# A graph transformer layer on one core: Gram product of the upper block triangle with transposed copies below, and a tail with its work spread anew over four engines

## What is computed

```python
xn = layernorm(x)
x = x + gnn(xn, edges) + mix(xn)
x = x + ffn(layernorm(x))

def mix(x):                     # no softmax: linear attention over all nodes
    q, k, v = x @ Wq.T + bq, x @ Wk.T + bk, x @ Wv.T + bv
    return (q @ k.T * scale) @ v @ Wo.T + bo

def ffn(x):                     # each operand rounded to fp4 in blocks of 16
    gate, up = lin4(x, gate_w), lin4(x, up_w)
    return lin4(silu(gate) * up, down_w)
```

## Time and profile before

| | us |
|---|---|
| median of 3 runs | 1122.34 (1117.62 to 1124.64) |
| the profiled execution | 1125.02 |
| its span, first to last instruction | 1123.0 |
| PE busy | 970.6 (86%) |
| DVE busy | 869.0 (77%) |
| POOL busy | 593.5 (53%) |
| ACT busy | 532.4 (47%) |

### The profile page before, as it was taken

One profiled execution on the slowest core, in us unless ns is written; L12 is line 12 of the kernel. 1 busy time (PEld: TensorE's weight loads), 2 busy tenths in 40 slices (PEclk: granted clock), 3 DMA queues, 4 the chain that ended last, 5 costly groups with the idle time before them and its releaser, 6 DMA issues.

```text
span 1123.0 us, 10097 instructions
## 1 busy us (share of the span) xinstructions
PE 970.6 (86%) x2989; PEld 466.7 (42%) x2998; DVE 869.0 (77%) x1027; ACT 532.4 (47%) x1890; POOL 593.5 (53%) x577
## 2 busy tenths in 40 slices
PE   0798999997999999999999999998999947566754
PEld 0675544443494434434444444443444423222321
DVE  6989749493999999999999999986000387888795
ACT  0123213310788887887999989867000121111110
POOL 3223327455778777777778778772100163344332
PEclk9999999998969999999999999998999967777888
DMA  8104051243466533554355433580100000000001
GB/s 255 75 1 119 10 181 33 51 137 116 147 95 182 173 95 98 178 168 116 97 157 180 113 101 102 189 316 17 47 0 1 14 1 0 38 19 19 20 38 52
DMA packets 59461, 105.30 MB, mean 94 GB/s; under 512 B 24631, under 2 KB 32468, under 8 KB 59130
## 3 DMA queue, kind: packets, MB, share of 16 engines
q0 software_dynamic: 18560, 50.70, 17.2%
q1 hardware_dynamic: 40842, 53.92, 14.3%
HBM read 92.30 MB, written 12.45 MB: 93 GB/s over the span
## 4 chain that ended last, share of the span: by engine, by line
DVE 47%; PE 20%; POOL 16%; issue 9%; DMA 3%; SPq 2%; ACT 1%; POOLq 0%; DVEq 0%; ACTq 0%
PE acc L717 13%; POOL round_mem L511 10%; DVE z L1551 6%; DVE turned L1413 6%; DVE turned L1549 5%; DVE acc_sb L1421 5%; PE acc L890 3%; DVE round_mem L1172 3%; DVE round_mem L1171 3%; DVE round_mem L1170 2%; POOL round_mem L493 2%; DVE round_mem L1169 2%; PE acc L888 2%; DMA round_mem<-msg_table,idx 1%; DVE round_mem L1295 1%
## 5 line engine op out<-in xcount | busy, mean ns | idle before, releaser
L511 POOL DMA_INDIRECT round_mem<-msg_table,idx x352 | 338.9, 963 | 110.6 <-issue 84.5
L1106 ACT ACTIVATE round_mem<-round_mem,pz 128x65 f32<-128x65 f32 x1408 | 354.4, 398 | 14.1 <-DVE acc_sb L1421 10.7
L717 PE MATMUL acc<-wslot,big_a 128*128 128x512 f32 x512 | 226.3, 602 | 4.9 <-DVE big_a L1372 3.5
L717 PEld LDWEIGHTS acc<-wslot,big_a 128*128 128x128 f32 x512 | 97.8, 193 | 129.6 <-issue 118.9
L493 POOL TENSOR_TENSOR round_mem<-round_mem 128x1024 bf16<-128x1024 bf16 (+3 forms) x52 | 85.6, 1654 | 121.1 <-DVE round_mem L1173 76.0
L717 PE MATMUL acc<-big_a,xhat_t 128*128 128x512 f32 x320 | 140.8, 603 | 3.6 <-ACT xhat_t L1042 3.6
L1421 DVE TENSOR_REDUCE acc_sb<-round_mem 128x260 f32<-128x1820 f32 (+1 forms) x62 | 121.6, 1962 | 12.3 <-POOL round_mem L665 5.3
L1489 DVE TENSOR_TENSOR big_b<-acc,big_b 128x1024 f32<-128x1024 f32 x10 | 12.2, 1223 | 131.8 <-PE acc L890 131.8
L717 PE MATMUL acc<-wslot,big_b 128*128 128x512 f32 x256 | 111.1, 594 | 2.5 <-DVE big_b L1369 2.3
L1413 DVE TENSOR_TENSOR turned<-round_mem,turned 128x1560 f32<-128x1560 f32 (+1 forms) x62 | 105.4, 1700 | 6.5 <-DMA round_mem<-msg_table,idx 3.9
L717 PE MATMUL acc<-big_b,wslot 128*128 128x512 f32 x256 | 110.0, 592 | 0.0
(11 more groups left out here) (194 smaller groups left out, 1140.3 us busy)
## 6 DMA issues: line engine op xcount, KB each, us to landing
big_b<-in_x SPq DMA_DIRECT2D x18, 512.0 KB, 10.6
round_mem<-msg_table,idx POOLq DMA_INDIRECT x352, 2.8
out_x<-big_b SPq DMA_DIRECT2D x9, 512.0 KB
wslot<-in_wv_t SPq DMA_DIRECT2D x2, 2048.0 KB, 11.0
wslot<-in_wk_t SPq DMA_DIRECT2D x2, 2048.0 KB, 10.4
wslot<-in_wo_t SPq DMA_DIRECT2D x2, 2048.0 KB, 9.8
wslot<-in_wq SPq DMA_DIRECT2D x2, 2048.0 KB, 9.6
wslot<-in_gate_w SPq DMA_DIRECT2D x1, 2048.0 KB, 9.8
```

The source lines that it names most:

```text
L511: pool.indirect_dma_start(xg[g % 4][:, j, :], None, msg_table, bass.IndirectOffsetOnAxis(idx[:, c, j0 + j:j0 + j + 1], 0)).then_inc(xg_in[ ...
L717: mm = nc.tensor.matmul(o(acc[:, n % 4, :]), a, b, start=first, stop=last)
L1106: ins = nc.scalar.activation(to[:, :, j], xg[g % 4][:, j, h * HR + 1:(h + 1) * HR], ACT.Copy, scale=pz[:, g % 2, j, h:h + 1])
```

## The change

Three parts.

1. **Gram.** The order becomes m = 4,0,5,1,6,2,7,3 for half 1 and 0,4,1,5,2,6,3,7 for half 0. Of each group only the blocks on or above the diagonal are multiplied (10 matmuls of 512, 384, 256 or 128 columns); the blocks below are transposed from rows that ACT has already copied, behind a wait on group i-2. Weight pieces are turned behind other groups.
2. **Planner and weight stage.** PRODUCTS_AT 212 in place of 240; six `p` groups, not three, are taken before round 0; the sum of column sums moves from piece 10 to piece 8; SP loads the two bias rows at q == 8 once `gram` is done.
3. **Tail.** The residual goes to ACT: a Copy out of PSUM that sums along the row, a Copy of one column (mean), a Square that sums. Bias and x are added to the base product by POOL ahead of `up` (`add_up`, two instructions a chunk, for chunks 0 to 8 before the loop). DVE does three of the four block multiplications, POOL keeps that of the rounded hidden values. `up` runs three chunks ahead, and the orders of the loops change.

```diff
-GRAM = [(m, 1) for m in range(8)] + [(m, 0) for m in range(8)]
+GRAM = [(m, 1) for m in (4, 0, 5, 1, 6, 2, 7, 3)] + [(m, 0) for m in (0, 4, 1, 5, 2, 6, 3, 7)]
-TURNED_AFTER = {("lin", 0): 2, ("gram", 2): 3, ("gram", 6): 4, ("gram", 7): 5, ("gram", 8): 6, ("gram", 10): 7,
-                ("gram", 15): 8, ("p", 1): 9, ("p", 2): 10, ("p", 3): 11}
+TURNED_AFTER = {("lin", 0): (2,), ("gram", 2): (3,), ("gram", 6): (4,), ("gram", 8): (5,), ("gram", 10): (6,), ("gram", 12): (7,),
+                ("p", 2): (8,), ("p", 4): (9,), ("p", 6): (10, 11)}
...
                 if q == 8:
                     sp.wait_ge(w_quantized, 2)
                     sp.dma_start(view(3), uses[3][1]).then_inc(w_in[1], 16)
-                sp.wait_ge(wq_taken, q + 1)
-                if q == 9:
-
                     sp.wait_ge(acc_full, index_of["gram", 15] + 1)
                     sp.dma_start(bv_bc, bv.rearrange("(a d) -> a d", a=1).to_broadcast([P, D])).then_inc(vb_in, 16)
                     sp.dma_start(bk_bc, bk.rearrange("(a d) -> a d", a=1).to_broadcast([P, D])).then_inc(vb_in, 16)
+                sp.wait_ge(wq_taken, q + 1)
...
+            def add_up(c):
...
+                nc.gpsimd.tensor_tensor(base[0:n, c, :], x_last if c == C - 1 else base[:, c, :], bias_bc[0:n, :], ALU.add).then_inc(summed_x, 1)
+                pool.wait_ge(summed_x, c + 1)
+                pool.wait_ge(acc_taken["act"], taken[index_of["base", ORDER["base"].index((c, 1))]])
+                nc.gpsimd.tensor_tensor(base_at[c][0:n], base_at[c][0:n], base[0:n, c, :].rearrange("p (k n) -> p k n", k=KB),
+                                        ALU.add).then_inc(base_done, 1)
...
                 pool.wait_ge(stats2_done, c + 1)
+                step(nc.gpsimd.tensor_scalar(small[:, c:c + 1], mean_var[:, c, 1:2], 1.0 / D, LN_EPS, ALU.mult, ALU.add))
                 step(nc.gpsimd.tensor_tensor(rstd[:, c:c + 1], small[:, c:c + 1], minus_half[:, 0:1], ALU.pow))
...
             for k in range(-1, C + 1):
...
+                if k == 1:
+                    add_up(C - 1)
+                if 0 <= k and k + 3 < C:
+                    invert_deviation(k + 3)
                 if 0 <= k - 1 < C:
                     pool.wait_ge(h_rounded, k)
                     by_block(h_bf[(k - 1) % 2], tail_factors[k % 2][0][:, D // QB:], I).then_inc(h_done, 1)
...
             up(1)
+            up(2)
             for k in range(-1, C + 1):
-                if k != 0 and max(k, 0) + 2 < C:
-                    up(max(k, 0) + 2)
-                if 0 <= k < C:
-                    gate_up(k)
+                if 0 <= k + 1 < C:
+                    turn_q(k + 1)
+                if 0 <= k and k + 3 < C:
+                    up(k + 3)
                 if 0 <= k - 1 < C:
                     down(k - 1)
                 if 0 <= k + 1 < C:
-                    turn_q(k + 1)
+                    gate_up(k + 1)
...
-        early = {index_of["p", i]: 257.0 + 2 * i for i in range(3)}
+        early = {index_of["p", i]: 232.0 + 6 * i for i in range(6)}
...
+            def residual(c):
+
+                act.wait_ge(x2_full, c + 1)
+                nc.scalar.activation(base[:, c, :].rearrange("p (a b) -> p a b", a=2), acc[0:NC, base_bank(c):base_bank(c) + 2, :], ACT.Copy,
+                                     accum_out=less_mean[:, c:c + 1]).then_inc(x2_done, 1)
...
+                nc.scalar.activation(squares, base[:, c, :], ACT.Square, bias=mean_var[:, c, 0:1],
+                                     accum_out=mean_var[:, c, 1:2]).then_inc(stats2_done, 1)
...
+            residual(1)
+            act.wait_ge(stats2_done, 2)
+            residual(2)
             for k in range(-1, C + 1):
                 if k + 2 < C:
                     normalize(k + 2)
+                if 0 <= k + 1 < C:
+                    turn_over(k + 1)
+                if 0 <= k and k + 3 < C:
+                    act.wait_ge(stats2_done, k + 3)
+                    residual(k + 3)
...
-                    if q >= 10:
-                        for i in ((0,), (1, 2))[q - 10]:
-                            take(index_of["p", i])
+                    for i in {8: (0,), 9: (1, 2), 10: (3, 4), 11: (5,)}.get(q, ()):
+                        take(index_of["p", i])
...
             def rows_rounded(c):
-                dve.wait_ge(q_spread, c + 1)
+                k = c - 1
+                sc8, inv = tail_factors[k % 2]
+                dve.wait_ge(tail_scaled, k + 2)
+                step(scaled(ln2[c % 2], inv[:, 0:D // QB], D))
                 if c >= 2:
                     dve.wait_ge(q_tp, c - 1)
-                round_to_fp4(ln2[c % 2], q_bf[c % 2], qa).then_inc(q_rounded, 1)
+                step(round_to_fp4(ln2[c % 2], q_bf[c % 2], qa))
+                scaled(q_bf[c % 2], sc8[:, 0:D // QB], D).then_inc(q_done, 1)
...
             for k in range(-1, C + 2):
                 if k <= C:
                     tail_scales(k)
-                if k + 2 < C:
-                    residual(k + 2)
+                if 0 <= k + 1 < C:
+                    rows_rounded(k + 1)
                 if 0 <= k - 2 < C:
                     finish(k - 2)
                 if 0 <= k - 1 < C:
                     hidden_rounded(k - 1)
-                if 0 <= k + 1 < C:
-                    rows_rounded(k + 1)
```

`turn_over` is the copy of the turned rows that stood in the loop before; `scaled` is the block multiplication on DVE; the parts of `group("gram", ...)` are these:

```diff
+                here = range(4 * h, 4 * h + 4)
+                own = max(m, 4 * h)
+                parts = [] if m > here[-1] else [
+                    (lambda a, o=own - 4 * h: a[:, o * P:], xhat[:, c, m * P:(m + 1) * P], xhat[:, c, own * P:(h + 1) * HALF],
+                     c == 0, c == C - 1) for c in range(C)]
+                mirrored = [(lambda a, k=k: a[:, (k - 4 * h) * P:(k - 4 * h + 1) * P], mat_a[:, k, m * P:(m + 1) * P], ident[:], None, None)
+                            for k in here if k < m]
+                group("gram", i, parts + mirrored, (len(parts), acc_taken["act"], taken[index_of["gram", i - 2]]) if mirrored else None)
```

More of the change, by code:

```diff
@@ L53 @@
 NH2 = NP // 5
[L54 removed]
+PRODUCTS_AT, GROUP_STEP = 212.0, {"p0": 26.0}
 ROUND_0_AT, ROUND_STEP = 268.0, 8.4
@@ L679, in _ @@
                     send_attention(c)
+            for c in range(C - 1):
+                add_up(c)
             for c in range(3):
-                add_bias(c)
-            invert_deviation(0)
+                invert_deviation(c)
             for k in range(-1, C + 1):
-                c = k + 1
-                if 0 <= k - 1 < C:
-                    pool.wait_ge(tail_scaled, k + 2)
-                    by_block(hidden, tail_factors[k % 2][1][:, D // QB:], I).then_inc(h_spread, 1)
-                if c < C:
-                    pool.wait_ge(tail_scaled, k + 2)
-                    by_block(ln2[c % 2], tail_factors[k % 2][1][:, 0:D // QB], D).then_inc(q_spread, 1)
-                if k + 2 < C:
-                    invert_deviation(k + 2)
+                if k == 1:
+                    add_up(C - 1)
+                if 0 <= k and k + 3 < C:
+                    invert_deviation(k + 3)
                 if 0 <= k - 1 < C:
@@ L704, in _, with group @@
             done = [0]
-            def group(kind, i, products):
+            def group(kind, i, products, behind=None):
                 n = index_of[kind, i]
@@ L712, in group @@
                     pe.wait_ge(acc_taken[groups[n - 4][2]], taken[n - 4])
-                for o, a, b, first, last in products:
+                for nth, (o, a, b, first, last) in enumerate(products):
+                    if behind and nth == behind[0]:
+                        pe.wait_ge(behind[1], behind[2])
                     if first is None:
@@ L782, in turn_due @@
             def turn_due(kind, i):
-                q = TURNED_AFTER.get((kind, i))
-                if q is not None:
+                for q in TURNED_AFTER.get((kind, i), ()):
                     turn_weights(q, q + 1)
@@ L1074, in _ @@
             for i in range(16):
-                if ("p", i) in TURNED_AFTER:
-                    piece(TURNED_AFTER["p", i])
+                for q in TURNED_AFTER.get(("p", i), ()):
+                    piece(q)
             act.wait_ge(order_done, 2)
@@ L1129, in _ @@
                 if 0 <= c < C:
-                    act.wait_ge(q_tp, c + 1)
+                    act.wait_ge(gu_full, c + 1)
                     if c >= 2:
-                        act.wait_ge(gu_full, c - 1)
-                    nc.scalar.copy(q_t[c % 2][:, :, 0:NC], tpb[:, 0, :].rearrange("p (k n) -> p k n", k=KB)[:, :, 0:NC]).then_inc(q_taken, 1)
+                        act.wait_ge(hid_done, c - 1)
+                    nc.scalar.activation(silu[c % 2], acc[0:NC, 2, :], ACT.Silu, scale=cscale[0:NC, 0:1]).then_inc(silu_done, 1)
         @block.vector
@@ L1564, in _ @@
                 take(n)
-            residual(0)
             for k in range(-1, C + 2):
```

98 lines of the change are left out of this document (43 added, 55 removed).

## The result

| | before | after |
|---|---|---|
| median of 4 runs | 1121.95 us (1117.62 to 1124.64) | 1086.65 us (1083.03 to 1088.84) |
| ratio | | 0.9686, 95% interval 0.9644 to 0.9727 |
| the profiled execution's span | 1123.0 | 1085.4 |
| end of `base` | 877.8 | 855.9 |
| from there to the end | 245.2 | 229.5 |

The kernel is 35 us faster, the forecast was 34 (1088). But the 37.6 us between the two traces are divided otherwise than forecast: 21.9 us come before the end of `base`, where I had 30, and 15.7 us from the tail, where I had 4. So the number was right by luck: two errors of opposite sign cancel, and the experiments ask about both.

A forecast was written before the change was run, and what follows sets the result against it. PE was taken to bound the kernel up to 877.8 us, then a circle over all engines. Savings of 15 + 10 + 6 - 1 = 30 us before the tail and 4 in it gave 1088 us; 8-in-10 range 1062 to 1105.

The forecast's parts named there:

- Gram's work: Gram stage: narrower groups and added transposes leave PE needing 23.4 us less.
- the surcharge: Gram stage: extra cost of 128-column matmuls, 40 records of them, 0 to 2.4 us, taken as 1.
- The wait for piece 4: Gram stage: behind group 6 PE waits 2.1 us for POOL to release weight piece 4 at 174.7.
- the head's 30 us: Everything up to the tail: 15 + 10 + 6 - 1 = 30 us less.
- The weights: Value-weight loads before the rounds: first starts at 208, PE idles 9 us; second at about 273, rounds start unmoved.
- The low clock: PE behind the two idle stretches before the rounds: lower clock costs 1 us.
- The planner: Rounds and `base`: earlier takes remove PE's waits, about 10 and 6 us.
- only Gram's share arrives: Rival, chance 0.18: new rounds don't fit, bank waits or unfilled groups remain, 30 becomes 15: 1103 us.
- The circle: Tail loop: PE, ACT's residual, POOL and ACT's copy in series take 22.3 us a chunk in place of 23.5.
- Start and end of the tail: Tail outside the steady chunks: start 7 us less, end 10 us more.
- Square needs no table of its own: Tail, denies the rival, chance 0.05, that Square needs its own table: two loads a chunk, 1106 us.
- the rival of full clock: Tail, chance 0.22: PE's clock stays up, circle 18.6 us, 22 us less, 1066 us.

The follow-up runs named there:

- x10: The changed kernel with the Gram product computed as before, twelve full groups in the old order and four of transposes: 1105.64 us, ratio 0.984.
- x9: The changed kernel with the 2048 KB load of the down weights held back until POOL has entered piece 4: 1075.50 us, ratio 0.959.
- x6: The changed kernel with POOL's multiplication of the rounded hidden rows put ahead of the inversion of the deviation in the tail loop: 1108.22 us, ratio 0.957.
- x5: The changed kernel again, unaltered, on a chip with longer rounds: 1122.85 us, ratio 0.9703.
- x3: The changed kernel with the planner's part taken back (PRODUCTS_AT 240, three early p groups, old turns of pieces 8 to 11): 1144.03 us, ratio 0.9884.
- x2: The kernel before with part 3 of the change, the new tail, alone: 1137.40 us, ratio 0.9828.
- x4: The changed kernel with weight piece 4 turned behind Gram group 7 in place of 6: 1124.05 us, ratio 0.9694.
- x7: The changed kernel with both value-weight loads moved earlier and PRODUCTS_AT 204 in place of 212: 1109.02 us, ratio 0.9572.
- x11: The changed kernel with both value-weight loads moved earlier, PRODUCTS_AT staying 212: 1073.97 us, ratio 0.957.
- x12: The changed kernel with early value-weight loads, PRODUCTS_AT 204, later down-weight load and POOL's two tail lines exchanged: 1052.16 us, ratio 0.9384.
- x8: The changed kernel with ACT's Square of the residual done twice per chunk in the tail: 1144.30 us, ratio 0.9867.

## Why the forecast came out as it did

**Gram's work** was right. The narrow groups take 6.62, 4.48 and 2.40 us for 20 records of 384, 256 and 128 columns; the surcharge is 0.12 - 0.11 = 0.01 a record, half a microsecond for the 40 records of 128 columns where I took 1. Gram's end is 24.2 us earlier with the narrow groups than with full ones (232.8 in x10, 208.6 in x9, POOL's wait 7 us in both); x10 began Gram 1.3 us later and x9 has PE's 1.7 us of wait in it, which leaves 24.6. Forecast 23.4.

**The wait for piece 4** is the step that failed in the head: forecast 2.1, measured 7.2. I took POOL's release at 174.7 from the earlier trace rows as if nothing ahead of it moved. But SP's load of the down weights did: it stands behind the store of piece 3, which PE turns behind gram group 2, and so began at 151.3 in place of 153.7, hence 6.2 us ahead of POOL's reduction, not 3.2. With that one load out of the way (x9) every later number of the head's chain is met. A quarter of the head's 30 us hung on a transfer that isn't in the diff, and on little time: in x6, where the same load began 4.5 us ahead of the reduction, POOL stood 7.2 us.

**The weights.** First load issued 213.9 for 208, second 277.2 for 273: both follow from piece 4 (x9: 206.9 and 270.3). PE stood 7.1 us for the first where I had 9; it takes 8.8 us from issue to use, not 11. The rounds begin 3.4 us later than before (POOL's second gather at 275.39, before 271.95), where I had them unmoved.

**The low clock** behind the idle stretches was under-sized: 1 us forecast, some 4 measured. `p` 8 and 9 take 16.6 us for 32 records, 0.52 each, where 0.43 is a record at full clock; from the begin of `p` 8 to 331.5 the changed kernel takes 41.3 us, the kernel before 37.1 for the same work. So of the 10 us of bank waits that go, 6 arrive at `base` (x9: 428.4 us from `p` 8 to there, before 434.4).

**The planner** was right: 10 and 6 us of waits for banks forecast, and the two stretches are 10.1 and 6.8 us shorter, with PE busy throughout. It holds for this chip: on the one with longer rounds PE is idle for 16.6 us between 344.9 and 757.7 in x5. x3 adds what I had not seen: without the new turns and takes Gram's share isn't smaller, it is nil. Of the rival "only Gram's share arrives" the premise was wrong, since no run shows such a share.

**The circle** was right in kind and 1.8 us too long: 20.5 for 22.3. PE 13.9 (14), ACT 2.6 (3.2, has a 1.23 that the Copy out of PSUM doesn't take: 1.02), POOL 3.1 (3.5), ACT's copy 0.7 with its hand-overs (1.3). DVE is busy 17.4 us a chunk, as forecast (17.5), so in the shorter chunk it is idle for 3.1 us, not 4 to 5. Five periods from the first `down` on bring 12.8 us (120.1 before, 107.2 after).

**Start and end of the tail** were both wrong in sign. I had the start 7 us faster; to the first `down` it is 6.5 us slower (57.2 us before, 63.7 after), in good part because ACT does residual 1 and 2 and a normalization ahead of the copy of the first turned rows (L1127 at 885.05, for which `gate_up` 0 waits 4.4 us). I had the end 10 us slower, since `down` is far back in the loop; from the sixth to the last `down` it is 9.2 faster (58.3 and 49.1). Once k + 3 passes the last chunk there is no `up` and no residual in the circle, and the last periods are 10.7, 17.3, 10.7 and 10.4. Of this loop, whose circle runs through a prefetch, the end is the cheap part. Sum: +6.5 - 12.8 - 9.2 - 0.2 = -15.7.

**Two forms of the same tail.** In the trace of the result the period from the first to the second `down` is 25.2 us, and the whole tail takes 229.5; in x9 and x10 it is the same within 0.1 us. In six other traces of this same tail (x2, x3, x4, x5, x7, x11) that period is 19.2 to 20.8 and the tail takes 224.0 to 225.5. In the long one POOL's three one-column instructions take 3.78 us from the first's start to the multiplication's, beside DVE's 1024-column ones, and in x5 1.07; PE's turn and `up` take 7.5 us against 5.8, at a lower clock. What decides between the two stays open. So the tail is worth 16 us in the pair of traces of the result and some 20 against the old one on the other chips, and differences of 4 us between single traces of it say nothing of an edit.

```profile
939.91 1.11 POOL L654 TENSOR_SCALAR small<-mean_var 128x1 f32<-128x1 f32 x1 [20.34 <-ACT round_mem L1119]
...
943.69 1.05 POOL L493 TENSOR_TENSOR round_mem<-round_mem 128x512 bf16<-128x512 bf16 x1
```

**Rivals.** Square needs no table of its own: one load of 1.28 us in the whole tail, at 886.06, ahead of Silu, with Squares on either side of it (the first at 864.5). The Trainium skill, "ScalarE: Activation LUTs", "Table sets: the hidden batching unit", prices a switch of sets; the trace shows none between Copy, Identity, Square and Silu. PE's clock in the tail was 0.83, between the forecast and the rival of full clock; in the middle of the tail of x6 and x12, whose idle stretch is shorter, it was 0.90 and 0.89.

## What to carry to other kernels

Cutting PE's work is worth what the turns, loads and takes hung on it let through: here nothing to be seen alone, 22 us with the schedule moved along, 28 when a transfer that had slid into another engine's way was held back. When an edit speeds up one engine, list what its queue neighbours now start earlier, DMAs included, and what they then run beside. And in a loop over several engines look for an instruction whose input is ready long before it runs; exchanging two lines on POOL brought 13 to 15 us.

## What the runs showed of the hardware

- POOL stands about 7 us without any semaphore between a reduction over partitions and the next ordinary instruction. At its second reduction it is 6.9 to 7.3 us in seven traces, 10.0 to 12.1 in seven others in which a 2048 KB load had begun 5.1 to 6.2 us ahead of the reduction (at most 4.5 us ahead, or not at all, in the first seven). The 4.5 is no limit that holds elsewhere. At the third reduction the first load of the value weights is near, and there POOL stands 9.6 to 11.7 us behind the reduction in the five traces in which that load began 2.9 to 4.8 us ahead of it; in six in which it began 7.8 to 13.4 us ahead, it is the wait in front of the reduction that has grown (7.7 to 10.2 us in place of 5.8 to 6.2). Both waits together are 13.1 to 13.6 us in the three traces without a load and 15.2 to 17.7 in these eleven. The changed kernel at that place:

```profile
218.55 0.38 POOL L517 PARTITION_ALL_REDUCE gmax<-wmax  x1 [6.06 <-issue]
228.48 3.82 POOL L493 TENSOR_TENSOR wslot<-wslot,round_mem 128x1024 f32<-128x1024 f32 x2 [9.55 <-issue]
```

- The Trainium skill, "GPSIMD Engine Reference", "Instruction dispatch", has the first call of a freshly loaded routine pay some 6 us with no instruction in the profile; the waits in front of the first reduction (5.8 to 6.5 us) and behind the second (about 7) fit it, and the traces show besides that such a wait can grow to 12.
- One-column instructions of POOL take 0.19 to 0.55 us beside DVE's small ones (x6) and 0.8 to 1.6 beside DVE's 1024-column ones (x8). The other way too: DVE's L1197 takes 1.23 us, and 2.11 while POOL multiplies (984.79 in the changed kernel). The Trainium skill, "SBUF — State Buffer", "Who interferes with whom", has a DVE instruction with two SBUF inputs contend with a GpSimd one that reads SBUF; these rows agree.
- Between chips the rounds differ: 7.9 and 8.5 to 8.6 us a round on average. The median round is 8.1 us on either; on the slower chips about every fifth is 2 to 6 us longer. Why stays open. The changed kernel's ratio to before is the same on both (0.9686 and 0.9703).
